# Three edits to a fused attention, FFN, mixer and quantised FFN kernel: when SyncE's stores of unpacked weights stand in line, an earlier split of the third projection weight, and a joined shift

## The reference: what is computed

```python
x = x + _layernorm(_L0_attn_ref(_layernorm(x), wq, wk, wv, wo))         # 32 heads of 16, rotary, causal
x = x + _layernorm(_L0_ffn_ref(_layernorm(x), gate_w, up_w, down_w, ...))  # 512 -> 1376 -> 512, rank 16 LoRA
x = x + _layernorm(_L1_attn_ref(_layernorm(x), Win, ..., Wout, bout))   # 4 layers: complex decaying scan + small MLP, width 64
x = x + _layernorm(_L1_ffn_ref(_layernorm(x), w1, s1, w2, s2, w3, s3))  # 512 -> 1376 -> 512, weights packed in 4 bits
```

```python
msb = w >> 4
lsb = (w & 15 ^ 8) - 8
g = jnp.concatenate([msb, lsb], axis=1).reshape(-1, GROUP)
deq = g.astype(s.dtype) * s[:, None]
```

## Time and profile before

| what | value |
|---|---|
| median of 3 runs | 858.61 us (854.3, 858.61, 858.93) |
| profiled execution | 855.57 us |
| its span in the trace | 853.8 us |
| instructions | 12935 |
| PE busy | 757.6 us, 89% of the span |
| DVE busy | 559.9 us, 66% |
| POOL busy | 444.7 us, 52% |
| ACT busy | 341.1 us, 40% |
| mean granted clock of PE | 0.973 of full |

### The profile page before, as it was taken

How to read it: one execution, slowest core, us unless ns; L and a number is a source line. 1 busy time by engine, 2 the same in 40 slices (tenths; PEclk the granted TensorE clock), 3 DMA queues, 4 the chain that set the end, 5 groups by cost and what they waited for, 6 DMA issues and landing times. The chain is left out here.

```text
span 853.8 us, 12935 instructions
## 1 busy us (share of the span) xinstructions
PE 757.6 (89%) x4483; PEld 549.6 (64%) x4483; DVE 559.9 (66%) x1211; ACT 341.1 (40%) x575; POOL 444.7 (52%) x595
## 2 busy tenths in 40 slices
PE   3799899999988976778999898889989989999995
PEld 2588655555555555557776676666767766688883
DVE  4444567777767368997447887888788787480015
ACT  5021156656666453323323433423344342433510
POOL 4333223454344234454747855855787584666732
PEclk9899889999999998989999999999999999999998
DMA  9002656554470021354674433542543121233301
GB/s 307 4 0 48 199 174 223 174 171 152 153 264 2 1 95 32 103 159 151 216 243 129 139 130 93 157 141 86 171 131 103 45 78 26 75 116 118 91 1 50
DMA packets 56945, 101.38 MB, mean 119 GB/s; under 512 B 13616, under 2 KB 17200, under 8 KB 54704
## 3 DMA queue, kind: packets, MB, share of 16 engines
q1 hardware_dynamic: 53616, 82.21, 31.2%
q0 software_dynamic: 2304, 16.78, 5.4%
q10 hardware_dynamic: 960, 1.57, 0.7%
HBM read 74.58 MB, written 27.00 MB: 119 GB/s over the span
## 5 line engine op out<-in xcount | busy, mean ns | idle before, releaser
L1509 PE MATMUL psum<-xt_hi,wgu_hi 128*128 128x512 f32 (+1 forms) x352 | 142.3, 404 | 0.0
L1509 PE MATMUL psum<-xt_hi,wgu_lo 128*128 128x512 f32 (+1 forms) x352 | 141.2, 401 | 0.0
L1509 PE MATMUL psum<-xt_lo,wgu_hi 128*128 128x512 f32 (+1 forms) x352 | 140.5, 399 | 0.0
L1299 DVE TENSOR_REDUCE negmax<-psum 128x2 f32<-128x1024 f32 (+3 forms) x128 | 104.3, 823 | 37.4 <-PE psum L1415 36.2
L783 POOL TENSOR_TENSOR wgu_lo<-raw,wgu_hi 128x512 fp32r<-128x512 f32 (+1 forms) x88 | 116.5, 1328 | 23.3 <-ACT wgu_hi L922 22.5
L820 POOL TENSOR_SCALAR_AFFINE_SELECT probs<-probs 128x256 f32<-128x256 f32 x128 | 52.4, 409 | 119.3 <-ACT probs L979 118.8
L979 ACT ACTIVATE probs<-psum 128x1024 f32<-128x1024 f32 (+3 forms) x128 | 89.5, 709 | 49.2 <-PE psum L1612 47.1
L783 POOL TENSOR_TENSOR wd_lo<-raw,wd_hi 128x512 fp32r<-128x512 f32 (+1 forms) x44 | 58.0, 1326 | 51.7 <-ACT wd_hi L929 51.7
L1143 DVE TENSOR_TENSOR hf<-sg,psum 128x512 f32<-128x512 f32 (+1 forms) x44 | 30.0, 681 | 77.6 <-PE psum L1509 55.5
L922 ACT ACTIVATE wgu_hi<-raw 128x512 fp32r<-128x512 f32 (+1 forms) x88 | 54.1, 617 | 61.3 <-PE psum L1506 41.0
L1509 PEld LDWEIGHTS psum<-xt_hi,wgu_lo 128*128 128x128 f32 (+1 forms) x352 | 66.0, 187 | 16.1
(11 more groups left out here) (208 smaller groups left out, 1574.1 us busy)
## 6 DMA issues: line engine op xcount, KB each, us to landing
raw<-full SPq DMA_DIRECT2D x60, 256.0 KB, 2.7
raw<-in_gu_t SPq DMA_DIRECT2D x40, 256.0 KB, 2.9
stage_w<-in_w SPq DMA_DIRECT2D x30, 256.0 KB, 3.0
full<-stage_w SPq DMA_DIRECT2D x30, 256.0 KB, 2.0
xt_hi<-turned POOLq DMA_DIRECT2D x7, 1024.0 KB, 5.2
xt_lo<-turned POOLq DMA_DIRECT2D x7, 1024.0 KB, 7.4
turned<-w_hi SPq DMA_DIRECT2D x52, 128.0 KB, 3.1
turned<-w_lo SPq DMA_DIRECT2D x26, 128.0 KB, 2.4
```

The lines of the kernel that those rows point to most:

```text
L1299: nc.vector.tensor_reduce(negmax[:, g, i, :], pair_of_banks(e)[:, :, 0:(i + 1) * P], AX_X, ALU.max, negate=True).then_inc(sem("row_max"), 1)
L1509: ins = nc.tensor.matmul(bank[q % 3][0:n, :], (wgu_hi, wgu_lo)[hi_w][:, q % 4, k, 0:n], XT[hi_x][:, k, ch * 512:ch * 512 + 512], start=ite ...
```

## The change

It has four edits.

1. The planner's costs: `q_shift` is put at 0.78 us in place of 0.7 (c < 2) and at 1.4 in place of 1.0 (c = 2), and `q_scale` has a lag of 3.0 in place of 0.15, so that its follower `q_keep` is planned 3 us behind it.
2. At the start DVE splits the third projection weight in its step t = 3, right behind the second, in place of t = 4.
3. `q_shift` for c = 2 is two instructions on 512 columns in place of four on 128: a left shift by a tensor of amounts, broadcast along each block, then, behind a wait for it, a right shift by 28 for all.
4. The table `shifts` holds amounts that suit this.

```diff
-            put("DVE", 0.7 if c < 2 else 1.0, "q_shift", m, c, after=(("q_in", m, c),), rank=3)
-            put("DVE", 0.85, "q_scale", m, c, after=(("q_shift", m, c),), rank=3)
+            put("DVE", 0.78 if c < 2 else 1.4, "q_shift", m, c, after=(("q_in", m, c),), rank=3)
+            put("DVE", 0.85, "q_scale", m, c, after=(("q_shift", m, c),), rank=3, lag=3.0)
...
-                if 2 <= t <= 4:
-
-                    dve.wait_ge(sem("w_split_hi"), t - 1)
-                    nc.vector.tensor_tensor(w_lo[:, t - 2, :, :], RAW[t - 2], w_hi[:, t - 2, :, :].bitcast(F32), ALU.subtract).then_inc(sem("w_split"), 1)
+                for j in {2: (0,), 3: (1, 2)}.get(t, ()):
+                    dve.wait_ge(sem("w_split_hi"), j + 1)
+                    nc.vector.tensor_tensor(w_lo[:, j, :, :], RAW[j], w_hi[:, j, :, :].bitcast(F32), ALU.subtract).then_inc(sem("w_split"), 1)
...
-                        for k in range(4):
-                            w = stage_w[0:n, q % 2, k * P:(k + 1) * P].bitcast(I32)
-                            ins = nc.vector.tensor_scalar(w, w, shifts[0:n, k, 0:1], shifts[0:n, k, 1:2], ALU.logical_shift_left, ALU.arith_shift_right)
+                        w = stage_w[0:n, q % 2, :].bitcast(I32)
+                        by_block = w.rearrange("p (k h) -> p k h", k=KD)
+                        link(nc.vector.tensor_tensor(by_block, by_block, shifts[0:n, 0:KD, 0:1].to_broadcast([n, KD, P]), ALU.logical_shift_left))
+                        ins = nc.vector.tensor_scalar(w, w, shifts[0:n, 0, 1:2], None, ALU.arith_shift_right)
```

More of the change, by code:

```diff
@@ L1703 @@
         low = (F * e + np.arange(P)) % P >= GROUP4 if e < 4 else np.arange(P) * KD // GROUP4 % 2 == 1
-        sh[:, e, 0] = np.where(low, 28, 0)
-        sh[:, e, 1] = np.where(low, 28, 4)
+        sh[:, e, 0] = np.where(low, 28, 0 if e == 4 else 24)
+        sh[:, e, 1] = np.where(low, 28, 4 if e == 4 else 28)
     arr["shifts"] = sh
```

## The result

The changed kernel takes 843.66 us in the median of 4 runs (842.52 to 845.46); the kernel before, run beside it on the same chip, 858.32 us in the median of 4 (854.3 to 858.93). The ratio is 0.984, 95% interval 0.982 to 0.987, so the change saves 1.6%, some 14 us.

What follows compares the result with a forecast made beforehand. PE, busy 89% of 853.8 us, was taken as the bound, waiting behind 400 us for DVE's small mixer steps. Terms -7.2 + 0.5 + 1.5 = -5.2 us, from a mean of 856.9, gave 851.7 us; 8-in-10 range 845 to 857.5.

Steps and rivals of the forecast that it cites:

- Edit 2, the third weight: At the start, the earlier split removes PE's 5.3 us wait for `w_lo` and 1.9 us of half clock: -7.2 us.
- Edit 3, the joined shift: In 11 packed tiles, the shift pair costs DVE +1 us in the mean, of which PE sees half: +0.5 us.
- Edit 1, SP's line: Stores later in SP's queue let loads go first, but PE doesn't wait for these loads: costed at nothing.
- the hole ahead of the fourth `merged`: PE's 7.30 us hole in front of 365.94, waiting for the third `merge` from a busy DVE: stays, with its half clock.
- Last the mixers: Tiles leave the first mixer (4.7 us back) and enter the second (9.5 us cost at most); taken as a 1.5 us loss.
- the slope: Between the two mixers' stretches: 5.5 points of PE idle time for 7 points of DVE busy time.
- the sign of its being wrong: The prediction is wrong if, among other signs, the mixers' PE idle time moves by more than 5 us in sum.
- (c): Better order: first mixer gives back 4.7 us, second has room; -11.9 us, some lost again, 846 us; chance 0.15.
- (a): Second mixer becomes DVE bound at 93%, costing the slope's +4.8 us or a little more: 856 us; chance 0.20.
- (b): Slower: six tiles' 12.6 us all become PE idle in the second mixer, nothing back in the first: 862 us; chance 0.07.
- (d): The hole at the start doesn't close: gain 3.6 us and not 7.2, so 855 us; chance 0.08.
- (e): PE's clock falls elsewhere; low-clock stretches like 101 to 115.2 change by some us either way; no separate chance given.

Runs made afterwards that it cites:

- f1_sp_only: Kernel before with each `q_keep` 3 us later in the plan's order, only SP's order differing: 856.99 us, 0.999 of before.
- f2_sp_back: Planner's new costs and lag alone, with each `q_keep` moved back 2.85 us in SP's line: 850.28 us, 0.992 of before.
- e2_planner: Kernel before with only the planner's numbers changed (0.78, 1.4, lag 3.0), the shifts still four: 849.80 us, 0.991 of before.
- The short kernels: Packed tiles' DVE steps cut to 2 columns in the orders of before, lag alone and planner's edit: 0.977, 0.988 and 0.974 of before.
- g4_lag4: Kernel before with planner costs 0.78 and 1.4 and a lag of 4.0, four separate shifts: 0.999 of before.
- h2_lag_short: Order of the lag of 3.0 alone (old costs), packed tiles' DVE steps cut to 2 columns: 0.988 of the kernel before.
- g3: Kernel before with planner costs 0.78 and 1.4 and a lag of 2.0, four separate shifts: 1.005 of before.
- e5_lag_only: Kernel before with only the lag of 3.0 in the plan, old costs 0.7 and 1.0, four separate shifts: 1.009 of before.
- e6_costs_only: Kernel before with only the costs 0.78 and 1.4 in the plan, old lag 0.15, four separate shifts: 1.001 of before.
- h1_before_short: Kernel before, in its own order, with the packed tiles' DVE steps cut to 2 columns: 0.977 of before.

## Why the prediction was wrong, step by step

**Edit 2, the third weight, -7.2 us: right.** Measured alone 0.9%: 7.7 us by the ratio, 7.0 by the medians; in the trace of the changed kernel 6.9. Both parts are there, the wait of 5.3 us and the half clock behind it: the clock is 1.00 in 20 to 40, where it was 0.83. The 0.4 us that are missing in the trace lie ahead of the hole, where PE came to full clock two products later than in the trace of before. The wait for `w_lo` is gone. The attention's first product comes at 88.1 us where it was 96.6, of which 1.5 are the earlier start.

**Edit 3, the joined shift, +0.5: right within what can be measured.** 1.001 [0.999, 1.002]. The groups of the changed kernel, for the earlier trace rows:

```profile
L1163 DVE TENSOR_TENSOR stage_w<-stage_w,shifts 128x512 int32<-128x512 int32 x10 | 9.6, 961 | 3.9 <-DMA stage_s<-in_scale 3.8
L1164 DVE TENSOR_SCALAR stage_w<-stage_w,shifts 128x512 int32<-128x512 int32 x10 | 8.6, 857 | 0.4
```

The pair takes 0.96 + 0.86 = 1.8 us in the mean, as estimated. The price of the four shifts was misread, though: the busy time of a group counts overlapping instructions once (40 of 0.494 us are 19.8, the row says 17.3 busy), so the 1.86 us of the earlier trace rows already were what a tile took, and nothing was to be taken off for overlap. So the join costs DVE nothing: 20.3 us in all (with 0.7 and 1.4 for the tile of 96 rows) where it was 17.3 + 3.2 = 20.5. Undisturbed the pair takes 0.69 and 0.49:

```profile
380.82 0.69 DVE L1163 TENSOR_TENSOR stage_w<-stage_w,shifts 128x512 int32<-128x512 int32 x1
381.54 0.49 DVE L1164 TENSOR_SCALAR stage_w<-stage_w,shifts 128x512 int32<-128x512 int32 x1
```

**Edit 1, SP's line at nothing: right.** `f1_sp_only` and `f2_sp_back` show it from both sides. That the hole ahead of the fourth `merged` remains was right as well.

**Edit 1, "Last the mixers": this step failed.** It counted tiles moved out of one stretch and into the other, turned each into a share of DVE's time, and that by a slope between two stretches into PE idle time, and took a loss of 1.5 us. Measured is a gain of 0.95%, 8 us. The first mixer gave back more than the 4.7 us of the slope, 5.8 us (13.1 to 7.3) in the changed kernel and 7.6 in `e2_planner`. The second, booked with up to 9.5 us of loss, gave back 2.1 and 2.5. So PE's idle time in the two moved by 7.9 and 10.1 us in sum, above the 5 us that the prediction named as the sign of its being wrong.

Two things in that step were wrong. It held the rest of DVE's work fixed and the stretches at their length: it put DVE at 80% and 93%, and the changed kernel has 80.79 / 97 = 83% and 78.61 / 94 = 84%. And the slope was not a law. In the second mixer DVE's share rose from 79% to 84%, and PE's idle share fell from 8.4% to 6.1%, where the slope has it rise. The slope came from two stretches that differ in more than DVE's load: the first mixer runs beside the second half of the first FFN and the second beside the first half of the last FFN, with other work for PE to fill in.

What the runs show in its place: the time hangs on the order of all engines' steps in and around the mixers, not on SP's line, not on how many tiles stand in a stretch, and not on DVE's time there. Orders with about the same tiles per mixer range from 0.991 to 1.009, partly by PE's waits and partly by its clock. Which feature of the planner's order is the good one is not shown. The short kernels rule out that it is the tiles' arithmetic alone.

**The rivals.** (c), the better order, named the right stage and the right sign, 846 us, and still stopped 2 us short, since it had the second mixer giving nothing. (a) rests on the failed slope and (b) on all the added tile time becoming PE idle time; the second mixer, where idle time fell, refutes both. (d) did not happen. (e) did not happen between these two kernels, whose mean clocks are 0.973 and 0.974: the low clock at the beginning of the attention is there in both. Among the neighbouring orders the clock did fall elsewhere, and PE was busy up to 11.8 us longer (`g4_lag4`), more than the few us that (e) allowed for. The changed kernel at the beginning of the attention, 92 to 110 us:

```profile
92.00:95.00 3.00, 2.45 (x21) 1.60 (x21) 2.93 (x6) 0.00 (x0) 0.00 (x0) 0.79 0.97 248
95.00:107.00 12.00, 12.00 (x72) 7.45 (x72) 6.74 (x13) 5.59 (x8) 2.77 (x6) 0.50 0.76 265
107.00:110.00 3.00, 3.00 (x31) 1.77 (x31) 2.49 (x3) 1.60 (x3) 0.82 (x2) 0.93 0.44 102
```

**The range.** Seven settings of three numbers gave times from 0.991 to 1.009 of before, with no rule that I could find. A reshuffle by the planner is a draw of about 8 us either way here, and the range allowed 6 up and 7 down around a sum that also had to hold the rest. Only one of the seven, the one in the change, is clearly faster than before. So the forecast got its direction from edit 2; for edit 1 nothing in the prediction could have given it.

**What stays open.** Which steps make the planner's order good, and which cost the order of the lag alone its 1.1%, is not settled; `h2_lag_short` says only that the latter isn't the tiles' arithmetic. What in an order lowers the clock is open. Nor was it tried whether the planner's order is the best near it; no run that computes the whole program beat the changed kernel.

## What to carry to other kernels

Where a scheduler writes the order, a changed cost or lag isn't a local edit: it reshuffles every engine, and here its effect couldn't be had by counting how many steps each stretch holds. Price such an edit as a draw whose spread is measured by a few neighbouring settings (here 1.8% from best to worst), and keep the best by measurement, not by which setting sounds right. When two orders are compared, read PE's busy time and its clock beside its idle time: an order can wait less and still take longer, as `g3` and `g4` do. The hole that waited for an engine busy 96% of its stretch was not filled by moving steps, neither on the late engine nor on the waiting one; it moved. The hole that waited for a step whose inputs had long been there, on an engine with slack, closed fully, and gave back the half clock behind it as well.

## What the runs showed of the hardware

**Small DVE steps take up to eight times as long beside a POOL step.** In the changed kernel, DVE's timeline where it makes tables:

```profile
357.50 0.69 DVE L1134 TENSOR_TENSOR raw<-raw,psum 128x512 f32<-128x512 f32 x1
...
358.79 0.17 DVE L1326 TENSOR_TENSOR high_turn<-turn_tmp 128x16 f32<-128x16 f32 x1
359.00 1.30 DVE L1327 TENSOR_TENSOR turn_tmp<-high_turn 128x16 f32<-128x16 f32 x1
360.23 0.16 DVE L1328 TENSOR_TENSOR turn_tmp<-high_turn 128x16 f32<-128x16 f32 x1
360.42 1.14 DVE L1329 TENSOR_TENSOR high_turn<-turn_tmp 128x16 f32<-128x16 f32 x1
```

and POOL's at the same time:

```profile
357.37 1.27 POOL L788 TENSOR_TENSOR h_lo<-hf,h_hi 128x512 fp32r<-128x512 f32 x1 [5.67 <-ACT h_hi L943]
358.98 1.28 POOL L783 TENSOR_TENSOR wd_lo<-raw,wd_hi 128x512 fp32r<-128x512 f32 x1 [0.35 <-ACT wd_hi L929]
360.24 1.29 POOL L783 TENSOR_TENSOR wgu_lo<-raw,wgu_hi 128x512 fp32r<-128x512 f32 x1
```

A step of 16 columns takes 0.16 us, and 1.30 when it begins just behind POOL's split of 1.28: it ends 0.04 us after it. The merge at 357.50, one of whose inputs is in PSUM, takes its usual 0.69 beside a POOL step of 1.27. The Trainium skill (SBUF — State Buffer, Terms, shared port pair) has the two engines take one pair of SBUF ports under an exclusive lock, held for the whole instruction, so that the loser is blocked and not slowed in proportion; the trace agrees, 1.30 for 0.16. By this a small move in the order can change the lengths of DVE's steps too, and they do differ: the same 1211 instructions keep DVE busy for 554.8 us in `e2_planner` and for 567.9 in `g3_lag2`. That alone doesn't rank the orders: `e5_lag_only` has 559.5 us at a ratio of 1.009 and `e6_costs_only` 563.8 at 1.001. How much of the spread of the seven settings comes from it was not tested.

**A DVE step of 2 columns is held up as long as one of 16.** In `h1_before_short` the shifts and scales have 2 columns. DVE's timeline shows both lengths next to each other:

```profile
418.12 0.28 DVE L1159 TENSOR_SCALAR stage_s<-stage_s,shifts 128x2 int32<-128x2 int32 x1
418.44 1.14 DVE L1165 TENSOR_TENSOR stage_s<-stage_s 128x2 f32<-128x2 int32 x1
419.50 1.33 DVE L1159 TENSOR_SCALAR stage_s<-stage_s,shifts 128x2 int32<-128x2 int32 x1
420.87 0.16 DVE L1165 TENSOR_TENSOR stage_s<-stage_s 128x2 f32<-128x2 int32 x1
```

Of the 66 steps, 51 take 0.15 to 0.65 us, and 15 take 1.04 to 1.39. Each of those 15 lies beside a POOL step of 128x512 (1.0 to 1.6 us long) and ends within 0.03 us of its end. The 15 make 18.1 of the 31.3 us; the other 51 take 0.26 us each in the mean, with next to nothing to work on. The two together are why only 36 of 68 us went when nearly all columns did.
